# Attention: output halves joined by an accumulating transfer, and one maximum of 768 columns at the unit's end

## Chip, cores and metric

One NeuronCore of a Trainium2 chip. The metric is the device time of one execution in microseconds (us).

## The reference

A transformer block on an input of 48 x 48 positions (2304 tokens) and 384 channels, in fp32: layer norm, attention with 12 heads of 32 channels and decomposed relative positions, projection, residual; then layer norm and a mixture of 8 experts with the best 2 gates. What matters here is the attention:

```python
qkv = x @ qkv_w + qkv_b            # x: layer norm of the input, 2304 tokens
q, k, v = ...                      # 12 heads, 32 channels each
attn = einsum('bqd,bkd->bqk', q * scale, k)
bias = rel_h[..., :, None] + rel_w[..., None, :]      # from q and two tables
attn = softmax(attn + bias, axis=-1)                  # 2304 x 2304 per head
out = einsum('bqk,bkd->bqd', attn, v)
return out @ proj_w + proj_b
```

## The kernel before, in words

The stages run one after another: q, k and v with layer norm; relative-position products; attention (`phase_attention`); projection; gates; experts. Only `phase_attention` changes.

**Precision.** Values are kept as a high part in fp32r and the rest as a low part. The values of v stand as 65 columns per key tile: 32 of high parts, 32 of low parts, and one of ones for the softmax's sum (`VW = 2 * HD + 1`). So the output of a head in `o_t` has 65 rows, and the rows 0 to 31 and 32 to 63 must be added: that is the join of the halves.

**Units.** A head has 3 query blocks of 768 queries (`QB`), and each block goes over 18 key tiles of 128 keys (`TILES`): 54 units a head, 648 in all. For a unit TensorE does, in its own order written out in `head`: the scores of the unit three later (`scores`, four matmuls of 384 columns into `ps_s`, two PSUM buffers), the product of the unit's weights with v (`pv`, four matmuls into `ps_o`, high and low weights), and two matmuls of 384 columns for the row maxima of later queries (`half`, into `ps_m`). These belong to the next head's maxima, 42 of 54 units ahead (`chunk_at`, `SHIFT = 12`); the last head has them in its first 12 units only. In the last unit of a block `pv` comes ahead of the scores.

**ScalarE** takes each unit's scores twice: exp to `p_hi` (L846) and exp to `p_f` (L852), whose two buffers come free by `lo_done` of the unit two earlier. **The low part** `p_lo = p_f - p_hi` (`low`, L598) is VectorE's for two units of three, and POOL's for every third (`POOL_EVERY = 3`). `pv` waits for it. VectorE's `head` takes the maximum of the first half (`reduce_half`, L897), then the low part of the unit two later, then the maximum of the second half. `negated` (L892) makes the negative maximum of a block once in 18 units; TensorE transposes it (L757) in the unit three before a block's end, inside `scores`, ScalarE copies it (L848) between its two exponentials, SP stores it (L642) and loads it into `query_rest` (`load_max`).

**The end of a block.** ScalarE and VectorE copy one half of the columns each from `ps_o` to `o_t` (L861, L912); two buffers `o_t`. POOL's `joined` runs after its low part of the sixth unit of the next block: it copies the rows 32 to 63 to `o_low` (L719) and adds them to the rows 0 to 31 in `o_s` (L721). SP stores `o_s` to `o_d` and the row of sums to `sums_d` (`store`, L650 and L651), after `load_max` of the same block.

**SP** issues all transfers of the stage in one order: `rest(h)` loads keys and values of the next head, then, for each block, `load_rest` (about 2.1 MB, the queries with low parts, each read for six variants), `load_max` and `store`; `start` loads the next but one head's `query_hi` and `key_hi`. All of it is on one hardware queue.

Of the kernel before, what the change touches and what calls it, by code (L numbers as in the profile page):

```python
# [21 lines left out]
HEADS = 12  # L22
# [488 lines left out]
def phase_attention(nc, qk_hi_d, qk_lo_d, rel_hi_d, rel_lo_d, v_d, m_d, o_d, sums_d, key_hi0, key_rest0, room):  # L511
# [11 lines left out]
    with ExitStack() as ctx:  # L523
# [22 lines left out]
        o_low = [sb(f"o_low{i}", [HD, 2, TB]) for i in range(2)]  # L546
        o_s = [sb(f"o_s{i}", [HD, 2, TB]) for i in range(2)]
# [23 lines left out]
        o_go = sem("o_go")  # L571
        low_moved = sem("low_moved")
        o_sum = sem("o_sum")
        ot_out = [sem(f"ot_out{i}") for i in range(2)]
        all_in = sem("all_in")
# [33 lines left out]
        def _(sp):  # L609
# [44 lines left out]
            def start(h, par, last=False):  # L654
                if not last:

                    sp.wait_ge(s_ok, UNITS * h + LEAD)
                    load_hi(h + 1, 1 - par)
                load_max(h, 2)
# [24 lines left out]
            start(0, 0)  # L684
# [4 lines left out]
            for g in range(2):  # L689
                sp.wait_ge(ot_out[g], 32 + 32 * QBLOCKS * OALL_HEADS // 2)  # L690
# [5 lines left out]
            for g in range(2):  # L696
                sp.wait_ge(ot_out[g], 32 + 32 * QBLOCKS * HEADS // 2)
# [3 lines left out]
        def _(pool):  # L701
            for g in range(2):
                pool.sem_inc(ot_out[g], 32)
# [6 lines left out]
            def joined(h, par, b, last_one):  # L710

                g = (QBLOCKS * par + b) % 2
# [10 lines left out]
            FIRST = 3 * POOL_EVERY  # L723

            def head(h, par, last=False):
                for idx in range(FIRST - 1, UNITS + FIRST - 1, POOL_EVERY):
# [13 lines left out]
            head(HEADS - 1, 1, last=True)  # L740

        @block.tensor
        def _(pe):
# [32 lines left out]
            def head(h, par, last=False):  # L776
                for k in range(UNITS):
# [61 lines left out]
        def _(act):  # L839
# [14 lines left out]
            def head(h, par, last=False):  # L854
                for k in range(UNITS):
                    if k % TILES == TILES - 1:
# [3 lines left out]
                        act.wait_ge(ot_out[g], out_count(h, par, b))  # L860
# [4 lines left out]

            def out_count(h, par, b):
                return 32 * ((QBLOCKS * par + b) // 2) + 32 * QBLOCKS * half(h, par) + 32

            def half(h, par):
                return (h - par) // 2  # L870
# [16 lines left out]
        def _(dve):  # L887
# [6 lines left out]
            def reduce_half(count, s, c):  # L894
                dve.wait_ge(mm_ok, 2 * count + c + 1)
                col = s % 3 * 2 + c
                dve.tensor_reduce(mx[s // TILES][:, s // 3 % 6, col:col + 1], ps_m[:, c, 0:TB], AX.X, ALU.max).then_inc(mx_ok, 1)  # L897

            def reduce_both(s, ps):
                dve.wait_ge(mm_ok, 2 * s + 2)  # L900
                col = s % 3 * 2
                dve.tensor_reduce(mx[s // TILES][:, s // 3 % 6, col:col + 2], ps[:, :, 0:TB], AX.X, ALU.max).then_inc(mx_ok, 2)
                negated(s, s)

            def head(h, par, last=False):
                for k in range(UNITS):
                    if k % TILES == TILES - 1:
# [3 lines left out]
                        dve.wait_ge(ot_out[g], out_count(h, par, b))  # L911
# [4 lines left out]
                    if maxima:  # L916
                        reduce_half(number, s, 0)
# [7 lines left out]
            def out_count(h, par, b):  # L925
                return 32 * ((QBLOCKS * par + b) // 2) + 32 * QBLOCKS * half(h, par) + 32

            def half(h, par):
                return (h - par) // 2
# [3 lines left out]
            for s in range(UNITS - SHIFT):  # L933
                reduce_both(s, [ps_m, ps_s[:, 0:2, :], ps_s[:, 2:4, :]][s % 3])
# [960 lines left out]
```

## Time and profile before

| | us |
|---|---|
| median of 3 runs | 2444.59 |
| lowest and highest | 2442.36, 2445.06 |
| profiled execution, its own time | 2443.99 |
| profiled execution, its span | 2442.2 |

| engine | busy us | share of the span |
|---|---|---|
| TensorE | 2083.4 | 85% |
| TensorE weight loads (beside it) | 1821.8 | 75% |
| VectorE | 1536.9 | 63% |
| ScalarE | 1505.6 | 62% |
| POOL (GpSimd) | 984.6 | 40% |

The attention runs from about 340 to 1625 us of the span. Shares over the whole span average stages with different limits, so the argument needs the views of that stage. In the timelines a row is one instruction or several alike (x2), with its start, its time, engine, line, and what it writes and reads; in brackets stands the idle time of the engine ahead of it and who ended it. A matmul's row is longer than the time to the next, since matmuls overlap.

### The profile page before, as it was taken

Reading aid. Unit: us, or ns where it says so; the run is one execution under the profiler, and the core shown is the slowest. Engines: PE = TensorE matmul, PEld = TensorE weight load, DVE = VectorE, ACT = ScalarE, POOL = GpSimd, SP = SyncE. Lnnn points to the kernel's source line nnn. Section 1 sums busy time; section 2 is a strip of 40 time slices with the busy share of each in tenths; the row PEclk is TensorE's granted clock in tenths of the full one; section 3 lists DMA queues with packets and bytes.
Section 4 is the critical chain, followed back from the end, with each engine's and each line's share of the span. In section 5 each row is a group of like instructions: output and inputs, shape, how many; then the busy total and the mean of one; then the engine's idle time right before and its main releaser. Section 6 shows DMA issues by size and latency. Waiting matters only on the chain. (4 is left out here: it accounts for less than half of the span.)

```text
span 2442.2 us, 34255 instructions
## 1 busy us (share of the span) xinstructions
PE 2083.4 (85%) x11132; PEld 1821.8 (75%) x11132; DVE 1536.9 (63%) x2321; ACT 1505.6 (62%) x2533; POOL 984.6 (40%) x645
## 2 busy tenths in 40 slices
PE   7833259999999999999999999967579999999998
PEld 7822138888888888888888888746368888989997
DVE  5555368989999898999988989747633426030000
ACT  3344308877787778777877877851235555555554
POOL 0020023434443443444344434447055656565553
PEclk9955559999999999999999999978679999999999
DMA  6788783444553554446345543333143435121111
GB/s 207 234 163 197 158 158 81 88 93 81 97 113 63 106 101 93 78 86 120 74 89 99 97 94 66 91 120 116 60 138 104 126 96 169 27 56 30 27 27 20
DMA packets 90710, 247.01 MB, mean 101 GB/s; under 512 B 8824, under 2 KB 43096, under 8 KB 85156
## 3 DMA queue, kind: packets, MB, share of 16 engines
q1 hardware_dynamic: 80640, 227.11, 40.5%
q0 software_dynamic: 8944, 16.91, 4.0%
q8 instruction: 101, 1.65, 0.3%
q10 hardware_dynamic: 960, 0.80, 0.1%
q14 instruction: 65, 0.53, 0.1%
HBM read 182.81 MB, written 61.98 MB: 100 GB/s over the span
## 5 line engine op out<-in xcount | busy, mean ns | idle before, releaser
L897 DVE TENSOR_REDUCE mx<-ps_m 128x1 f32<-128x384 f32 x1212 | 644.7, 552 | 110.7 <-PE ps_m L748 102.5
L598 POOL TENSOR_TENSOR p_lo<-p_f,p_hi 128x768 fp32r<-128x768 f32 x216 | 397.8, 1842 | 764.9 <-ACT p_f L852 764.9
L846 ACT ACTIVATE p_hi<-ps_s 128x768 fp32r<-128x768 f32 x648 | 528.3, 815 | 176.3 <-PE ps_s L762 172.8
L852 ACT ACTIVATE p_f<-ps_s 128x768 f32<-128x768 f32 x648 | 525.5, 811 | 62.8 <-DVE p_lo L598 60.0
L748 PE MATMUL ps_m<-key_hi,query_hi 128*128 128x384 f32 x1240 | 430.7, 354 | 122.4 <-DVE mx L897 81.5
L598 DVE TENSOR_TENSOR p_lo<-p_f,p_hi 128x768 fp32r<-128x768 f32 x432 | 508.5, 1177 | 37.6 <-ACT p_f L852 36.6
L748 PEld LDWEIGHTS ps_m<-key_hi,query_hi 128*128 128x128 f32 x1240 | 237.0, 193 | 179.1 <-DVE mx L897 106.5
L759 PE MATMUL ps_s<-query_hi,key_hi 128*128 128x384 f32 x1296 | 341.6, 345 | 11.4 <-DMA query_rest<-m_d 9.3
L772 PE MATMUL ps_o<-p_hi,val 128*65 128x384 f32 x1296 | 335.7, 340 | 3.9 <-POOL p_lo L598 3.7
L762 PE MATMUL ps_s<-query_rest,key_rest 121*128 121x384 f32 x1296 | 335.8, 341 | 0.0
L772 PE MATMUL ps_o<-p_lo,val 128*65 128x384 f32 x1296 | 334.9, 340 | 0.0
L1675 POOL TENSOR_TENSOR h_lo<-h_f,h_hi 128x512 fp32r<-128x512 f32 x129 | 185.6, 1438 | 258.7 <-ACT h_hi L1803 256.4
L759 PEld LDWEIGHTS ps_s<-query_hi,key_hi 128*128 128x128 f32 x1296 | 234.5, 191 | 21.0 <-issue 10.3
L762 PEld LDWEIGHTS ps_s<-query_rest,key_rest 121*128 121x128 f32 x1296 | 241.0, 192 | 0.0
L1787 ACT COPY z_sb<-ps_z 128x512 f32<-128x512 f32 x129 | 75.7, 587 | 265.9 <-PE ps_z L1729 265.9
L1729 PE MATMUL ps_z<-w_ring,xg_hi 128*128 x774 | 223.8, 397 | 4.7 <-POOL xg_lo L1671 4.7
L1750 PE MATMUL ps_o<-w_ring,h_hi 128*128 x1032 | 214.5, 350 | 11.7 <-POOL h_lo L1675 11.7
L772 PEld LDWEIGHTS ps_o<-p_lo,val 128*65 128x65 f32 x1296 | 177.6, 137 | 52.1
L772 PEld LDWEIGHTS ps_o<-p_hi,val 128*65 128x65 f32 x1296 | 178.5, 138 | 31.5 <-POOL p_lo L598 5.6
L1750 PEld LDWEIGHTS ps_o<-w_ring,h_hi 128*128 128x128 f32 x1032 | 175.5, 188 | 15.2 <-issue 15.2
L1729 PEld LDWEIGHTS ps_z<-w_ring,xg_hi 128*128 128x128 f32 x774 | 144.7, 189 | 28.9 <-issue 5.1
L1797 ACT ACTIVATE h_f<-ps_h,b_sb 128x128 f32<-128x128 f32 x516 | 147.8, 369 | 6.3 <-issue 0.8
(247 smaller groups left out, 2355.0 us busy)
## 6 DMA issues: line engine op xcount, KB each, us to landing
query_rest<-rel_lo_d SPq DMA_DIRECT2D x36, 864.0 KB
query_rest<-qk_lo_d SPq DMA_DIRECT2D x36, 576.0 KB
query_rest<-qk_hi_d SPq DMA_DIRECT2D x36, 576.0 KB
rel_lo_d<-out_lo SPq DMA_DIRECT2D x6, 1728.0 KB, 33.1
query_hi<-rel_hi_d SPq DMA_DIRECT2D x12, 864.0 KB, 18.5
w_raw__19855<-w_u SPq DMA_DIRECT2D x12, 768.0 KB, 5.3
w_raw__19856<-w_u SPq DMA_DIRECT2D x12, 768.0 KB, 4.6
w_raw__19857<-w_u SPq DMA_DIRECT2D x12, 768.0 KB, 4.4
```

The costliest lines, as they stand in the source:

```text
L598: engine.tensor_tensor(p_lo[r][:], p_f[idx % 2], p_hi[r][:].bitcast(F32), ALU.subtract).then_inc(lo_done(0, idx)[0], 1)
L748: pe.matmul(ps[:, c, 0:TB], query_hi[tp][:, tile], key_hi[tp][:, keys], start=True, stop=True).then_inc(mm_ok, 1)
L759: pe.matmul(ps_s[:, bank + c, 0:TB], key_hi[par][:, j * P:(j + 1) * P], query_hi[par][:, b * QB + c * TB:b * QB + (c + 1) * TB], start=Tru ...
L762: last = pe.matmul(ps_s[:, bank + c, 0:TB], key_rest[par][:, j * P:(j + 1) * P], query_rest[b][:, j // 3, c * TB:(c + 1) * TB], start=Fals ...
L772: last = pe.matmul(ps_o[0:VW, c, 0:TB], val[par][:, j, :], part[r][:, c, :], start=(j == 0 and part is p_hi), stop=(j == TILES - 1 and par ...
L846: act.activation(p_hi[r][:], ps_s[:, bank:bank + 2, 0:TB], ACT.Exp).then_inc(hi_ok, 1)
L852: act.activation(p_f[idx % 2], ps_s[:, bank:bank + 2, 0:TB], ACT.Exp).then_inc(f_ok, 1)
L897: dve.tensor_reduce(mx[s // TILES][:, s // 3 % 6, col:col + 1], ps_m[:, c, 0:TB], AX.X, ALU.max).then_inc(mx_ok, 1)
L1675: pool.tensor_tensor(h_lo[u % H_RING][:], h_f[u % 2][:], h_hi[u % H_RING][:].bitcast(F32), ALU.subtract).then_inc(hlo_ok, 1)
L1729: last = pe.matmul(ps_z[:, u % 2, :], v[s % 2][:, k, :], moe.ring[:, cols], start=(n == 0), stop=(n == 8))
L1750: last = pe.matmul(ps_o[:, s % 2, 0:C], v[u % H_RING][:, b, :], moe.ring[:, cols], start=(c == 0 and n == 0), stop=(c == CHUNKS - 1 and n ...
L1797: last = act.activation(h_f[u % 2][:, b, :], ps_h[:, u % 2, b, :], ACT.Gelu, bias=bias)
```

## The change

Two parts. First, POOL's copy and sum and the buffers `o_low` and `o_s` go. SP stores the high rows of `o_t` to `o_d` right after the block's two copies, ahead of `load_max` and behind `load_rest`; when they have landed (`high_out`), POOL issues a transfer that adds the low rows of `o_t` to the same place in `o_d` (`accum_op`), after its low part of the ninth unit of the next block (`JOIN = 8`). The copies to `o_t` wait for that transfer (`low_out`) of the block two before. Second, TensorE issues both matmuls for the maxima at the unit's end, behind one wait, and VectorE takes one maximum of both (`reduce_both`, 768 columns), with the low part after it.

```diff
             def store(h, par, b):
                 g = (QBLOCKS * par + b) % 2
-                sp.wait_ge(o_sum, QBLOCKS * h + b + 1)
-                sp.dma_start(o_d[bass.ds(h * HD, HD), b * QB:(b + 1) * QB], o_s[g][:].rearrange("r c n -> r (c n)")).then_inc(ot_out[g], 16)
+                sp.wait_ge(acc_a, QBLOCKS * h + b + 2)
+                sp.wait_ge(acc_d, QBLOCKS * h + b + 2)
+                sp.dma_start(o_d[bass.ds(h * HD, HD), b * QB:(b + 1) * QB], o_t[g][0:HD, :, :].rearrange("r c n -> r (c n)")).then_inc(high_out[g], 16)
...
                     sp.wait_ge(s_ok, UNITS * h + TILES * (b + 1))
                     load_rest(h + 1, b)
+                    store(h, par, b)
                     if b < 2:
                         load_max(h + 1, b)
-                        store(h, par, b)
-                start(h + 1, 1 - par, h == HEADS - 2)
-                store(h, par, 2)
+                if h < HEADS - 2:
+                    sp.wait_ge(s_ok, UNITS * (h + 1) + LEAD)
+                    load_hi(h + 2, par)
+                load_max(h + 1, 2)
...
-                pool.wait_ge(acc_a, QBLOCKS * h + b + 2)
-                pool.wait_ge(acc_d, QBLOCKS * h + b + 2)
-
-                pool.wait_ge(*lo_done(h + (b == QBLOCKS - 1), (TILES * (b + 1) + 2 * POOL_EVERY - 1) % UNITS) if not last_one else lo_done(h, UNITS - 1))
-                pool.sem_inc(o_go, 1)
-                pool.tensor_copy(o_low[g][:], o_t[g][HD:2 * HD, :, :]).then_inc(low_moved, 1)
-                pool.wait_ge(low_moved, QBLOCKS * h + b + 1)
-                pool.tensor_tensor(o_s[g][:], o_t[g][0:HD, :, :], o_low[g][:], ALU.add).then_inc(o_sum, 1)
+            def joined(n):
+
+                h, b = n // QBLOCKS, n % QBLOCKS
+                g = n % 2
+                pool.wait_ge(high_out[g], 16 * (n // 2) + 16)
+                pool.dma_start(o_d[h * HD:(h + 1) * HD, b * QB:(b + 1) * QB], o_t[g][HD:2 * HD, :, :].rearrange("r c n -> r (c n)"),
+                               accum_op=ALU.add).then_inc(low_out[g], 16)
...
-                    for b in range(QBLOCKS):
-                        if idx == TILES * (b + 1) + 2 * POOL_EVERY - 1:
-                            joined(h, par, b, last and b == QBLOCKS - 1)
+                    n = QBLOCKS * h + idx // TILES - 1
+                    if idx % TILES == JOIN and idx < UNITS and n >= 0:
+                        joined(n)
...
                     if maxima:
                         if s == 0:
-
                             pe.wait_ge(hi_in[tp], 48 * ((h + 1) // 2 + 1))
 
-                        pe.wait_ge(mx_ok, number - 1)
-                        half(tp, s, 0, ps_m)
...
                     if maxima:
                         pe.wait_ge(mx_ok, number)
-                        half(tp, s, 1, ps_m)
+                        for c in range(2):
+                            half(tp, s, c, ps_m)
...
                         act.wait_ge(pv_ok, UNITS * h + k + 1 + RING)
-                        act.wait_ge(ot_out[g], out_count(h, par, b))
+                        if QBLOCKS * h + b >= 2:
+                            act.wait_ge(ot_out[g], 16 * ((QBLOCKS * h + b) // 2))
+                            act.wait_ge(low_out[g], 16 * ((QBLOCKS * h + b) // 2))
                         act.copy(o_t[g][:, 0, :], ps_o[0:VW, 0, 0:TB]).then_inc(acc_a, 1)
...
-            def reduce_both(s, ps):
-                dve.wait_ge(mm_ok, 2 * s + 2)
+            def reduce_both(count, s, ps):
+                dve.wait_ge(mm_ok, 2 * count + 2)
                 col = s % 3 * 2
                 dve.tensor_reduce(mx[s // TILES][:, s // 3 % 6, col:col + 2], ps[:, :, 0:TB], AX.X, ALU.max).then_inc(mx_ok, 2)
...
                     if maxima:
-                        reduce_half(number, s, 0)
+                        reduce_both(number, s, ps_m)
                     up, idx = unit_at(par, k, LOW_LEAD)
                     if not (last and up != par) and idx % POOL_EVERY < POOL_EVERY - 1:
                         low(dve, UNITS * h + k + LOW_LEAD, up, idx)
                     if maxima:
-                        reduce_half(number, s, 1)
                         negated(number, s)
```

VectorE's copy to `o_t` gets the same two waits as ScalarE's.

## Rows read from the trace of the kernel before

**Rows 1.** Two stretches of one block: span, busy times, granted clock, DMA share, GB/s.
```profile
963.03:997.67 34.64, 32.17 (x183) 28.44 (x182) 31.82 (x51) 27.91 (x39) 14.26 (x8) 1.00 0.37 68
1066.99:1103.27 36.28, 33.82 (x183) 29.82 (x182) 32.07 (x51) 27.87 (x39) 14.29 (x8) 0.95 0.36 65
```
**Rows 2.** Waits, 380 to 1560 us: who for whom, us in total, times, longest.
```profile
PE ps_m L748 <- DVE mx L897: 81.5, 66, 2.3
```
**Rows 3.** Timeline of undisturbed units: start, us, engine, line, operation.
```profile
1018.80 0.34 PE L748 MATMUL ps_m<-key_hi,query_hi 128*128 128x384 f32 x1
...
1019.00 0.81 ACT L846 ACTIVATE p_hi<-ps_s 128x768 fp32r<-128x768 f32 x1 [0.85 <-PE ps_s L762]
1019.17 0.56 DVE L897 TENSOR_REDUCE mx<-ps_m 128x1 f32<-128x384 f32 x1 [0.31 <-PE ps_m L748]
...
1019.71 0.81 ACT L852 ACTIVATE p_f<-ps_s 128x768 f32<-128x768 f32 x1
...
1021.44 0.81 ACT L852 ACTIVATE p_f<-ps_s 128x768 f32<-128x768 f32 x1
1021.45 0.95 DVE L598 TENSOR_TENSOR p_lo<-p_f,p_hi 128x768 fp32r<-128x768 f32 x1
1021.58 0.51 PE L759 MATMUL ps_s<-query_hi,key_hi 128*128 128x384 f32 x2
...
1022.31 1.02 DVE L897 TENSOR_REDUCE mx<-ps_m 128x1 f32<-128x384 f32 x2
1022.33 1.84 POOL L598 TENSOR_TENSOR p_lo<-p_f,p_hi 128x768 fp32r<-128x768 f32 x1 [5.85 <-ACT p_f L852]
...
1023.33 0.52 PE L759 MATMUL ps_s<-query_hi,key_hi 128*128 128x384 f32 x2
```
**Rows 4.** Timeline behind a join on POOL.
```profile
1013.86 3.44 DVE L598 TENSOR_TENSOR p_lo<-p_f,p_hi 128x768 fp32r<-128x768 f32 x1
...
1014.67 1.81 POOL L598 TENSOR_TENSOR p_lo<-p_f,p_hi 128x768 fp32r<-128x768 f32 x1
...
1017.33 0.81 ACT L852 ACTIVATE p_f<-ps_s 128x768 f32<-128x768 f32 x1 [1.81 <-DVE p_lo L598]
1017.82 0.45 PE L748 MATMUL ps_m<-key_hi,query_hi 128*128 128x384 f32 x1 [2.27 <-DVE mx L897]
```
**Rows 5.** Tile `o_t`, 380 to 1560 us: times, ns min/median/max, first and last start.
```profile
L721 POOL TENSOR_TENSOR o_s<-o_t,o_low x33: 2417/2433/2445, 415.0 to 1539.0; 32x768 f32<-32x768 f32 x33
```
**Rows 6.** Timeline at a block's turn.
```profile
1002.16 0.54 DVE L912 COPY o_t<-ps_o 65x384 f32<-65x384 f32 x1
...
1004.73 0.45 PE L748 MATMUL ps_m<-key_hi,query_hi 128*128 128x384 f32 x1 [0.20 <-DVE mx L897]
```
**Rows 7.** Timeline: second halves before and after the transposed maxima.
```profile
1030.15 0.33 PE L748 MATMUL ps_m<-key_hi,query_hi 128*128 128x384 f32 x1
...
1032.03 0.34 PE L748 MATMUL ps_m<-key_hi,query_hi 128*128 128x384 f32 x1
```
**Rows 8.** Tile `out` (experts), from 1600 us: POOL's accumulating transfers, issue ns, landing us.
```profile
L1680 POOL DMA_INDIRECT out<-y_sb,sidx x43: 1560/1594/2124, 1825.9 to 2433.7; - x43
...
DMA to landing us min/median/max: 3.0/4.2/5.7
```
**Rows 9.** A stretch of 4 us behind the loads of a head's first block.
```profile
1050.00:1054.00 4.00, 1.72 (x10) 1.39 (x9) 3.62 (x5) 1.32 (x3) 1.16 (x1) 1.00 0.81 100
```
**Rows 10.** Tile `mx`, 340 to 460 us: maxima of 768 columns ahead of the first head.
```profile
L902 DVE TENSOR_REDUCE mx<-ps_m x7: 947/948/949, 340.4 to 356.2; 128x2 f32<-128x768 f32 x7
```
**Rows 11.** Timeline of the experts: two-input operations of VectorE and POOL that start close together.
```profile
1797.52 2.74 DVE L1035 TENSOR_TENSOR w_ring<-w_raw__19855,w_ring 128x1536 fp32r<-128x1536 f32 x1
1797.63 1.00 POOL L1671 TENSOR_TENSOR xg_lo<-xg_f,xg_hi 128x384 fp32r<-128x384 f32 x1
...
1803.83 1.76 DVE L1035 TENSOR_TENSOR w_ring<-w_raw__19857,w_ring 128x1536 fp32r<-128x1536 f32 x1
1804.12 2.33 POOL L1671 TENSOR_TENSOR xg_lo<-xg_f,xg_hi 128x384 fp32r<-128x384 f32 x1 [5.49 <-ACT xg_f L1782]
```

More of the change, by code:

```diff
@@ L545, in phase_attention @@
         o_t = [sb(f"o_t{i}", [VW, 2, TB]) for i in range(2)]
-        o_low = [sb(f"o_low{i}", [HD, 2, TB]) for i in range(2)]
-        o_s = [sb(f"o_s{i}", [HD, 2, TB]) for i in range(2)]
         ps_s = ctx.enter_context(nc.psum_tensor("ps_s", [P, 4, 512], F32))
@@ L570, in phase_attention @@
         acc_d = sem("acc_d")
-        o_go = sem("o_go")
-        low_moved = sem("low_moved")
-        o_sum = sem("o_sum")
+        high_out = [sem(f"high_out{i}") for i in range(2)]
         ot_out = [sem(f"ot_out{i}") for i in range(2)]
+        low_out = [sem(f"low_out{i}") for i in range(2)]
         all_in = sem("all_in")
@@ L648, in store @@
                 g = (QBLOCKS * par + b) % 2
-                sp.wait_ge(o_sum, QBLOCKS * h + b + 1)
-                sp.dma_start(o_d[bass.ds(h * HD, HD), b * QB:(b + 1) * QB], o_s[g][:].rearrange("r c n -> r (c n)")).then_inc(ot_out[g], 16)
+                sp.wait_ge(acc_a, QBLOCKS * h + b + 2)
+                sp.wait_ge(acc_d, QBLOCKS * h + b + 2)
+                sp.dma_start(o_d[bass.ds(h * HD, HD), b * QB:(b + 1) * QB], o_t[g][0:HD, :, :].rearrange("r c n -> r (c n)")).then_inc(high_out[g], 16)
                 sp.dma_start(sums_d[bass.ds(h, 1), b * QB:(b + 1) * QB],
                              o_t[g][VW - 1:VW, :, :].rearrange("r c n -> r (c n)")).then_inc(ot_out[g], 16)
[L654 to L659, printed above, removed]
             def rest(h, par):
@@ L683, in _ @@
             sp.wait_ge(hot_ok, HOT_STEPS)
-            start(0, 0)
+            sp.wait_ge(s_ok, LEAD)
+            load_hi(1, 1)
+            load_max(0, 2)
             for h in range(loop_heads):
@@ L689, in _ @@
             for g in range(2):
-                sp.wait_ge(ot_out[g], 32 + 32 * QBLOCKS * OALL_HEADS // 2)
+                sp.wait_ge(ot_out[g], 16 * QBLOCKS * OALL_HEADS // 2)
+                sp.wait_ge(low_out[g], 16 * QBLOCKS * OALL_HEADS // 2)
             for c in range(KC):
@@ L696, in _ @@
             for g in range(2):
-                sp.wait_ge(ot_out[g], 32 + 32 * QBLOCKS * HEADS // 2)
+                sp.wait_ge(ot_out[g], 16 * QBLOCKS * HEADS // 2)
+                sp.wait_ge(low_out[g], 16 * QBLOCKS * HEADS // 2)
             sp.wait_ge(all_in, 16 * KC)
@@ L701, in _ @@
         def _(pool):
-            for g in range(2):
-                pool.sem_inc(ot_out[g], 32)
             pool.memset(ident[:], 0.0).then_inc(ident_ok, 1)
@@ L708, in _ @@
             one_hots(pool, key_hi[1], key_rest[1], hot, hot_ok)
[L710 to L721 removed]
+            def joined(n):
[4 more added lines that the diff above has]
+                               accum_op=ALU.add).then_inc(low_out[g], 16)
             FIRST = 3 * POOL_EVERY
+            JOIN = 8
             def head(h, par, last=False):
@@ L740, in _ @@
             head(HEADS - 1, 1, last=True)
+            joined(QBLOCKS * HEADS - 1)
         @block.tensor
@@ L864, in head @@
                         exps(h + (up != par), up, idx, turned_at(k, last))
[L866 to L870, printed above, removed]
             act.sem_inc(acc_a, 1)
@@ L892, in negated @@
                     dve.tensor_reduce(neg_m[s // TILES][:], mx[s // TILES][:], AX.X, ALU.max, negate=True).then_inc(neg_ok, 1)
[L894 to L897, printed above, removed]
-            def reduce_both(s, ps):
-                dve.wait_ge(mm_ok, 2 * s + 2)
+            def reduce_both(count, s, ps):
+                dve.wait_ge(mm_ok, 2 * count + 2)
                 col = s % 3 * 2
                 dve.tensor_reduce(mx[s // TILES][:, s // 3 % 6, col:col + 2], ps[:, :, 0:TB], AX.X, ALU.max).then_inc(mx_ok, 2)
-                negated(s, s)
             def head(h, par, last=False):
@@ L910, in head @@
                         dve.wait_ge(pv_ok, UNITS * h + k + 1 + RING)
-                        dve.wait_ge(ot_out[g], out_count(h, par, b))
+                        if QBLOCKS * h + b >= 2:
+                            dve.wait_ge(ot_out[g], 16 * ((QBLOCKS * h + b) // 2))
+                            dve.wait_ge(low_out[g], 16 * ((QBLOCKS * h + b) // 2))
                         dve.tensor_copy(o_t[g][:, 1, :], ps_o[0:VW, 1, 0:TB]).then_inc(acc_d, 1)
@@ L921, in head @@
                     if maxima:
-                        reduce_half(number, s, 1)
                         negated(number, s)
[L925 to L929, printed above, removed]
             dve.sem_inc(acc_d, 1)
@@ L933, in _ @@
             for s in range(UNITS - SHIFT):
-                reduce_both(s, [ps_m, ps_s[:, 0:2, :], ps_s[:, 2:4, :]][s % 3])
+                reduce_both(s, s, [ps_m, ps_s[:, 0:2, :], ps_s[:, 2:4, :]][s % 3])
+                negated(s, s)
             for idx in range(LOW_LEAD):
```

## The prediction

> **What bounds the kernel now.** I read the table of stretches first, because the change lies only in the attention stage. One block of 18 units, from one store of row maxima to the next, takes 34.64 us at a granted clock of 1.00, with TensorE busy for 32.17 us [rows 1]. The waits come next: TensorE's largest in this stage is for VectorE's maxima, 81.5 us in 66 waits, two in each of 33 blocks [rows 2]. Then the timeline, for what ends those waits. Undisturbed, a unit takes 1.75 us (scores at 1021.58 and 1023.33), which is 10 matmuls of 0.175, and TensorE never waits [rows 3]. So maxima as such are not the bound. 18 units are 31.5 us; the missing 3.14 us of a block are three disturbances:
>
> - The join of the output halves on POOL. VectorE's subtraction begins at 1013.86 and ends at 1017.30 in place of 0.95 later, and TensorE stands for 2.27 us [rows 4]. POOL's low part (1014.67 to 1016.48) had gone before it, behind the join's sum of 2.43 us [rows 4, 5]; VectorE ended 0.82 after POOL. Two-input subtractions on the two engines exclude each other.
> - The block's turn, where VectorE copies 0.54 us of output between its other work: a wait of 0.20 us is shown at the matmul after it [rows 6].
> - The transposed maxima: second half to second half 1.88 us instead of 1.75, so 0.13 [rows 7].
>
> Join and turn together therefore cost 34.64 - 31.50 - 0.13 = 3.01 us a block. Some blocks take longer: 36.28 us at a mean granted clock of 0.95, part of it at 1.2 GHz of the 2.4 [rows 1]. The 33 joins are 35.13 us apart on average (415.0 to 1539.0 in 32 steps) [rows 5], 0.49 more than 34.64, so the halved clock costs about 15.6 us in all.
>
> **The join, part by part.** Removed are 36 copies and 36 sums on POOL, 33 of them beside maxima. That takes away the 3.01 us less what the turn keeps: 33 x 3.01 = 99.3 us go. Added is one accumulating transfer a block, issued by POOL, for which the trace has only indirect ones, 1.59 us median, 1.56 to 2.12 [rows 8]. POOL has a low part every third unit, so every 5.25 us, and it takes 1.84 [rows 3], which leaves 3.4 us: the issue costs nothing, with at most 0 as gain. It waits for the high half's store, which on SP now stands behind the next head's big loads instead of ahead of them. In the worst block those keep the transfer engines busy for a share of 0.81 up to 1054 [rows 9]. POOL gets to that join 9 units, 4.8 us and the stalls below after the block's transposed maxima at 1030.15 [rows 7], about 1054.4; a wait of 1 us or so fits under the 3.4 less 1.6. At worst one block in three loses 1 us, 0 to 11 us; I take 0, since the cover is there. SP has queued behind the store only the next head's first loads and a row of maxima that isn't ready before. At the end of the stage the last join goes from 0.82 + 2.43 us of POOL to an issue of 1.59 with a landing of 4.2 [rows 5, 8] behind a store; I take 2 us more (0 to 4). In the last head, which mostly has no maxima, I take 2 us less.
>
> **The maximum, part by part.** One maximum of 768 columns takes 0.948 us [rows 10] instead of two of 0.55; instructions of VectorE back to back begin about 0.08 before their predecessor ends (1021.45 + 0.95 against 1022.31) [rows 3], so it is 0.87 of VectorE against two times 0.47. The work is near nothing less. What counts is the place. The maximum can begin only after both matmuls at the unit's end, and the subtraction, which stood between the two halves' maxima, comes after it. Time from the first scores matmul of a unit: the last of 10 matmuls starts at 1.575, its maximum 0.37 later (1018.80 to 1019.17) [rows 3], the subtraction at 1.95 + 0.87 = 2.82, ending at 3.77. In the old order it begins at about 1.6 (1021.45 in the unit begun 1.75 before 1021.58). VectorE needs 0.87 + 0.87 = 1.74 of 1.75: it fits with 0.01 to spare. The maximum ends at 2.90, TensorE wants it at 3.15. Fine as well.
>
> ScalarE's second exponential, which needs the buffer that this subtraction frees, starts 0.03 after its end (1017.30 to 1017.33) [rows 4], takes 0.81, and POOL starts 0.08 later (1022.25 to 1022.33) [rows 3]. So every third unit POOL's low part starts 0.95 + 0.03 + 0.81 + 0.08 - 1.75 = **0.12 us after** a subtraction of VectorE has begun. In the kernel before the two never meet. If VectorE goes first nothing is lost: POOL ends by 5.6 and its product is due at 5.95. If POOL goes first, it ends at 2.94 + 1.84 = 4.78, VectorE at 5.60, its next maximum at 5.52 + 0.95 = 6.47, and the halves start 0.15 later at 6.62 where 4.90 was due: **1.72 us**. Three places:
>
> - Transposed maxima: the matmuls come 0.13 later, ScalarE doesn't. 0.12 - 0.13: level, POOL first by 0.01. Price 1.72 - 0.13 = 1.59.
> - The turn, counted from the last half of the block's seventeenth unit: VectorE's maximum at 0.37, subtraction 1.24, copy 2.11, maximum 2.57, subtraction 3.44. TensorE goes on with the product and the scores, whose last matmul, the eighth, starts at 1.40; the exponentials follow at 1.77 and 2.48 (0.71 apart, 1019.00 to 1019.71) [rows 3], POOL at 2.48 + 0.81 + 0.08 = 3.37. POOL first by 0.07. The turn itself keeps 0.36 (maximum ends 3.52, halves at 3.68, due 3.32), and since POOL starts 3.37 - 0.18 = 3.19 into its unit, 0.25 later than the 2.94 above, the loss costs 1.72 + 0.25 - 0.36 = 1.61.
> - Four further meetings of a block, at 0.12.
>
> Who wins at 0.12? Two pairs of rows stand on its two sides: VectorE 0.11 us ahead (1797.52, 1797.63) was blocked and took 2.74 instead of 1.76, VectorE 0.29 ahead went first (1803.83, 1804.12) and POOL waited [rows 11]. The first case is impure: POOL had just ended another instruction, and back-to-back POOL instructions also pass a waiting VectorE [rows 4]. I take it that VectorE holds its place at 0.12 and keep the other end for the range.
>
> The Trainium skill, page "SBUF — State Buffer", section "Who interferes with whom", says that the shared port pair is an exclusive lock and goes to whoever issues first. By that rule the steady meetings are safe and both others are lost, which is my forecast; the 1797.52 row doesn't agree with it.
>
> **Sum**, on the profiled execution (2443.99 us, span 2442.2): less 99.3; plus 33 x (0.36 + 1.61 + 1.59) = 117.5; clock less 15.6, of which I give back 8, since stalls of 1.6 us come twice a block where 2.27 came once and nothing here shows whether they lower it (0 to 30); ends -2 and +2. 2443.99 + 10.6 = 2455. The median of the runs is 0.6 higher than the profiled one, which changes nothing.
>
> **Rivals.**
>
> 1. POOL also wins steady meetings. For it: the 1797.52 row. Against: its impurity. It decides from a lead needed by VectorE of over 0.12. Price 33 x 4 x 1.72 = 227 us: 2682 if all are lost. If starts scatter by more than what decides it, a share of them goes either way, 2500 to 2640. 0.24 for all, 0.20 for some.
> 2. The level meeting at the transposed maxima goes to VectorE: 33 x 1.59 less, and 4 of clock: 2399. 0.14.
> 3. VectorE wins at the turn too: 2399 - 53 - 4 = 2342. It needs VectorE to win from 0.07 behind. 0.05.
> 4. The stores land late and POOL's join holds its low part up (the change moves the wait instead of removing it): 11 us more at the bound above, more if the loads take longer: 2466 to 2500. 0.03.
>
> **Numbers.** My forecast has 0.34, with its own range 2436 to 2490 by clock and ends. About 0.2% is what a measurement can tell from no change, 2439.7 to 2449.5. Faster: 0.14 + 0.05 + 0.07 of the forecast's low end = 0.26. Same: 0.08 of it. Slower: 0.24 + 0.20 + 0.03 + 0.19 = 0.66. The range from 2395 to 2695 leaves out rival 3 and the edges.
>
> **What would show it.** After, POOL's sum and copy are gone; TensorE's waits for maxima are two a block, 1.4 to 1.6 us long, at the turn and at the transposed maxima, each with a subtraction of about 2.6 us on VectorE. A block is then about 35.1 us. If it is about 42, with a long subtraction every third unit, rival 1 holds; 32 would be rival 3. Long waits of POOL for the store before the join would be rival 4. A maximum well over 0.95 us would make the whole count wrong.

## The result and the profile after

The changed kernel takes 2352.43 us (median of 4 runs, 2351.75 to 2361.22) against 2443.58 (2442.36 to 2445.06) measured beside it: a ratio of 0.9635, 95% interval 0.9611 to 0.9659. It is 91 us faster where the forecast was 11 slower. The profiled execution is the slowest of the four, 2361.22 us with a span of 2359.1; it stands against 2443.99 and 2442.2 of before.

The costliest groups on VectorE and POOL (line, engine, operation, count | busy us, mean ns | idle before, releaser):

```profile
L595 POOL TENSOR_TENSOR p_lo<-p_f,p_hi 128x768 fp32r<-128x768 f32 x216 | 531.8, 2462 | 606.3 <-ACT p_f L840 606.3
L881 DVE TENSOR_REDUCE mx<-ps_m 128x2 f32<-128x768 f32 x620 | 592.4, 956 | 209.4 <-PE ps_m L738 207.0
...
L595 DVE TENSOR_TENSOR p_lo<-p_f,p_hi 128x768 fp32r<-128x768 f32 x432 | 424.1, 982 | 38.1 <-ACT p_f L840 37.0
```

POOL's low part is stretched to 2.46 us on average (1.84 undisturbed), VectorE's is not: 0.98, where an undisturbed one takes 0.95. So the meetings do take place, nearly every time, and POOL is the one that waits.

Stretches from one store of row maxima to the next (stretch: us, then busy us of PE, PEld, DVE, ACT, POOL, the granted clock, DMA share, GB/s): first 33 blocks in one, then a plain block, a block in which VectorE loses one meeting, and the block in which POOL's join waits longest. They answer to [rows 1].

```profile
397.89:1479.29 1081.40, 1060.20 (x5972) 919.76 (x5971) 912.68 (x1056) 920.71 (x1255) 518.38 (x231) 1.00 0.54 101
990.06:1022.15 32.09, 31.91 (x183) 27.75 (x182) 27.34 (x33) 27.92 (x39) 15.45 (x7) 1.00 0.56 114
1022.15:1056.11 33.96, 32.62 (x183) 27.78 (x182) 28.89 (x33) 27.89 (x40) 15.21 (x7) 1.00 0.42 73
595.02:633.61 38.59, 33.85 (x183) 29.19 (x183) 28.66 (x33) 27.87 (x39) 14.57 (x7) 0.96 0.55 95
```

A plain block takes 32.1 us instead of 34.64, 0.6 above the 31.5 of 18 undisturbed units. 33 blocks take 1081.4, which is 32.77 each, so 0.63 x 33 = 20.8 us lie in blocks longer than a plain one (32.14, the median of these). Cut at each store of row maxima, 16.5 of the 20.8 us are in ten blocks in which a join waits for its store (the fourth row has 6.45 of them), and 3.6 in two blocks that have another cause, of which the third row is one. In that row's block the join doesn't wait at all. VectorE's maximum starts 0.27 us late there, after idle time that the profile puts down to no wait ("issue"), and POOL passes it at the next steady meeting:

```profile
1049.60 0.96 DVE L881 TENSOR_REDUCE mx<-ps_m 128x2 f32<-128x768 f32 x1 [0.27 <-issue]
...
1050.25 1.84 POOL L595 TENSOR_TENSOR p_lo<-p_f,p_hi 128x768 fp32r<-128x768 f32 x1 [2.71 <-ACT p_f L840]
...
1050.47 2.43 DVE L595 TENSOR_TENSOR p_lo<-p_f,p_hi 128x768 fp32r<-128x768 f32 x1
```

The waits of the same stage (who for whom: us, times, longest); [rows 2] has no successor, since TensorE no longer waits for a maximum:

```profile
POOL o_d L708 <- DMA o_d<-o_t: 47.9, 13, 7.7
...
PE ps_o L762 <- POOL p_lo L595: 20.5, 44, 4.6
```

And the timeline from the transposed maxima through the turn (start, us, engine, line, operation):

```profile
1023.44 2.66 POOL L595 TENSOR_TENSOR p_lo<-p_f,p_hi 128x768 fp32r<-128x768 f32 x1 [2.78 <-ACT p_f L840]
1023.45 0.95 DVE L595 TENSOR_TENSOR p_lo<-p_f,p_hi 128x768 fp32r<-128x768 f32 x1
...
1025.47 0.51 PE L738 MATMUL ps_m<-key_hi,query_hi 128*128 128x384 f32 x2
...
1026.09 0.96 DVE L881 TENSOR_REDUCE mx<-ps_m 128x2 f32<-128x768 f32 x1 [0.79 <-PE ps_m L738]
...
1026.15 0.56 PE L762 MATMUL ps_o<-p_hi,val 128*65 128x384 f32 x2 [0.17 <-POOL p_lo L595]
...
1026.96 0.95 DVE L595 TENSOR_TENSOR p_lo<-p_f,p_hi 128x768 fp32r<-128x768 f32 x1
...
1027.83 0.55 DVE L892 COPY o_t<-ps_o 65x384 f32<-65x384 f32 x1
...
1028.52 0.81 ACT L840 ACTIVATE p_f<-ps_s 128x768 f32<-128x768 f32 x1
...
1029.16 0.94 DVE L595 TENSOR_TENSOR p_lo<-p_f,p_hi 128x768 fp32r<-128x768 f32 x1
...
1029.40 2.41 POOL L595 TENSOR_TENSOR p_lo<-p_f,p_hi 128x768 fp32r<-128x768 f32 x1 [3.31 <-ACT p_f L840]
```

At the first meeting POOL starts 0.01 us before VectorE and still waits. At the turn it starts 0.24 us after VectorE, not 0.07 before it.

### The profile page after: what moved, and what is told of

The parts are those of the page before. It is cut to its first block and busy times, and to the rows that moved or that the text cites. A ratio compares the mean times of both kernels' runs of the same rounds, so it can differ in the third digit from the quotient of the medians.

```text
span 2359.1 us, 34179 instructions
## 1 busy us (share of the span) xinstructions
PE 2058.6 (87%) x11132; PEld 1784.0 (76%) x11132; DVE 1393.5 (59%) x1715; ACT 1504.7 (64%) x2533; POOL 1026.6 (44%) x609
## 3 DMA queue, kind: packets, MB, share of 16 engines
q8 instruction: 101, 1.65, 0.3%
## 5 line engine op out<-in xcount | busy, mean ns | idle before, releaser
L595 POOL TENSOR_TENSOR p_lo<-p_f,p_hi 128x768 fp32r<-128x768 f32 x216 | 531.8, 2462 | 606.3 <-ACT p_f L840 606.3
L881 DVE TENSOR_REDUCE mx<-ps_m 128x2 f32<-128x768 f32 x620 | 592.4, 956 | 209.4 <-PE ps_m L738 207.0
L595 DVE TENSOR_TENSOR p_lo<-p_f,p_hi 128x768 fp32r<-128x768 f32 x432 | 424.1, 982 | 38.1 <-ACT p_f L840 37.0
L738 PE MATMUL ps_m<-key_hi,query_hi 128*128 128x384 f32 x1240 | 326.2, 344 | 40.9 <-DMA query_hi<-rel_hi_d 38.5
L738 PEld LDWEIGHTS ps_m<-key_hi,query_hi 128*128 128x128 f32 x1240 | 198.6, 190 | 101.0 <-DMA query_hi<-rel_hi_d 38.8
L762 PEld LDWEIGHTS ps_o<-p_hi,val 128*65 128x65 f32 x1296 | 173.2, 137 | 60.9 <-POOL p_lo L595 34.7
L469 PE MATMUL ps<-q_sb,tab 96*48 96x192 f32 x288 | 60.3, 365 | 106.0 <-DMA q_sb<-qk_lo_d 63.5
```

Source lines behind the costliest of these rows:

```text
L595: engine.tensor_tensor(p_lo[r][:], p_f[idx % 2], p_hi[r][:].bitcast(F32), ALU.subtract).then_inc(lo_done(0, idx)[0], 1)
L738: pe.matmul(ps[:, c, 0:TB], query_hi[tp][:, tile], key_hi[tp][:, keys], start=True, stop=True).then_inc(mm_ok, 1)
L762: last = pe.matmul(ps_o[0:VW, c, 0:TB], val[par][:, j, :], part[r][:, c, :], start=(j == 0 and part is p_hi), stop=(j == TILES - 1 and par ...
```

## Experiments

Lags below are POOL's start less VectorE's start, from the trace's start times to the nanosecond, for every pair of low parts that overlap; a "lost" meeting is one in which VectorE's subtraction took over 1.2 us. The 12 or 13 lost ones at the end of the last head, where no maxima run, are not counted. A steady meeting is one away from the turn and from the transposed maxima.

**Which half of the change brings the time?** First the join alone: the maxima stay where they were.

```diff
+                        pe.wait_ge(mx_ok, number - 1)
+                        half(tp, s, 0, ps_m)
...
-                        for c in range(2):
-                            half(tp, s, c, ps_m)
+                        half(tp, s, 1, ps_m)
...
-                        reduce_both(number, s, ps_m)
+                        reduce_half(number, s, 0)
...
+                        reduce_half(number, s, 1)
```

> Only the join is changed (accumulating DMA, new order on SP); the maxima stay two of 384, one in the middle of the unit. Theory A (the join's lock on VectorE was nearly all there was to gain, and the new place of the maximum costs at most the turn): VectorE's subtraction no longer stands 3.4 us behind POOL's sum, blocks near 31.5 + 0.13 + 0.3 = 31.9 us, and once a head a wait of about 1 to 2 us for the store as in the changed kernel: 2345 to 2360 us. Rival B (the maxima bring a good part of the 91 us, because with them the low part waits less for other work): over 2375 us.

Measured: 2352.63 us, ratio 0.9626 (0.9610 to 0.9642), the same as the whole change as far as the two intervals can tell. Theory A holds.

Then the maxima alone, with POOL's copy and sum kept (the same lines the other way round, in the kernel before).

> Only the maxima are changed (one of 768 columns, both matmuls at the unit's end); POOL keeps its copy and sum of 2.43 us. Theory A: the stall behind the join stays (about 2.3 us of TensorE a block), the meetings with POOL every third unit go to VectorE, which is 0.12 us ahead: 2435 to 2460 us. Rival B (the merged maximum gives slack by itself): under 2420 us. Rival C (with POOL's join beside it the meetings after it go to POOL for some units): over 2475 us.

Measured: 2464.62 us, ratio 1.0081 (1.0062 to 1.0101), 5 us beyond theory A's bound. The stall behind the join is still there:

```profile
1024.10 2.44 POOL L721 TENSOR_TENSOR o_s<-o_t,o_low 32x768 f32<-32x768 f32 x1
...
1025.63 3.50 DVE L598 TENSOR_TENSOR p_lo<-p_f,p_hi 128x768 fp32r<-128x768 f32 x1
1026.51 1.80 POOL L598 TENSOR_TENSOR p_lo<-p_f,p_hi 128x768 fp32r<-128x768 f32 x1
...
1029.18 0.57 PE L772 MATMUL ps_o<-p_hi,val 128*65 128x384 f32 x2 [2.08 <-DVE p_lo L598]
```

It is [rows 4] again: POOL's next low part, directly behind its sum, passes the subtraction that has waited since 1025.63. TensorE now misses the product instead of a maximum, for 2.08 us. Plain blocks take 34.74 us (34.64 before), and one with a stretch of halved clock 36.59 (36.28 before); of the 33 blocks 15 took over 36 us (first exponential to first exponential) where before it was 10. The two stretches:

```profile
1042.81:1077.55 34.74, 32.45 (x183) 27.76 (x182) 29.99 (x33) 27.93 (x40) 17.68 (x8) 1.00 0.51 102
1077.55:1114.14 36.59, 34.28 (x183) 29.09 (x182) 30.47 (x33) 27.92 (x40) 17.00 (x8) 0.95 0.35 65
```

So the merged maximum is worth nothing that shows beside the new join, and costs 23 us beside the old one (2464.62 less 2441.3, the kernel before in the same runs). Why it costs so much there was only partly found: 3.3 us are the 0.10 of each plain block, and the clock fell in 14 of the blocks instead of 10; the rest stays open.

**Is merging needed?** The changed kernel with two maxima of 384 behind both matmuls:

```diff
-                        reduce_both(number, s, ps_m)
+                        reduce_half(number, s, 0)
+                        reduce_half(number, s, 1)
```

> The changed kernel, but with two maxima of 384 columns back to back behind both matmuls in place of one of 768. 0.07 us more of VectorE in each unit; two units of three then ask 0.94 + 0.87 = 1.81 of it, the third 0.94, so on average it fits 1.75. The subtraction beside POOL's low part starts some 0.06 later, so its lead is 0.04 to 0.1 instead of 0.12. Theory A (VectorE goes first as long as it isn't behind by more than about 0.1): 2352 to 2362 us. Rival B (the merging is needed: the lead is used up and POOL goes first, up to four to six times a block at 1.7 us each): 2500 us or more.

Measured: 2347.17 us, ratio 0.9609 (0.9593 to 0.9625): rival B falls, and it is 5 us under theory A's range, though its interval overlaps the changed kernel's. The first of the two maxima starts before the second matmul has ended, so VectorE's subtraction starts 1.14 us after the unit's last matmul and not 1.32 (medians at the turn in this form and in the changed one). The steady lag goes from 0.12 to 0.08, as expected, and VectorE stays first.

**Is the join's wait for the high store worth removing?** All stores ahead of `load_rest` on SP, and the join three units later:

```diff
-            JOIN = 8
+            JOIN = 11
...
+                    store(h, par, b)
                     load_rest(h + 1, b)
-                    store(h, par, b)
```

> The changed kernel with the store of the high half put ahead of the next head's load_rest on SP's queue, and POOL's join three units later (5.25 us). Theory A (about 15 us of the changed kernel are POOL's waits for that store, once a head, and part of the clock behind the 4.56 us stall): the waits of TensorE for POOL's low part at these places are gone, 2335 to 2345 us. Rival B (the waits were hidden or come back as waits of the output copies for their buffer, which is now freed later): 2350 to 2356 us.

Measured: 2360.22 us (2355.13 to 2370.72), ratio 0.9678 (0.9651 to 0.9705): no gain, by the medians 8 us slower than the changed kernel, with intervals that just overlap. Neither theory named what came. POOL's waits in the 33 blocks are gone, but `query_hi` for the head after next comes late:

```profile
PE ps_o L762 <- DMA query_hi<-rel_hi_d: 9.3, 10, 1.4
```

In both kernels `load_hi` stands behind the third block's store on SP. What the edit moved is `load_rest`, which now also waits for that store. So SP issues the last of `load_hi` 10.6 us behind the block's store of row maxima instead of 7.5 (861.41 less 850.79, and 867.89 less 860.37), and it lands 17.4 us after its issue in place of 15.6 (medians). The edit moved the join too, so the run doesn't price the two parts one by one.

**What is a lost meeting worth, and where is the point of decision?** The forecast rests on both. An extra maximum on VectorE, of a constant tile and with its result unused, delays the subtraction that meets POOL, by its width:

```diff
                     if not (last and up != par) and idx % POOL_EVERY < POOL_EVERY - 1:
+                        if idx % POOL_EVERY == 1:
+                            dve.tensor_reduce(spare_mx[:, 0:1], ident[:, 0:8], AX.X, ALU.max)
```

> The changed kernel with one small extra maximum (8 columns of a constant tile, result unused) on VectorE ahead of the subtraction that meets POOL's low part (unit index 1 modulo 3). It delays that subtraction by an estimated 0.07 to 0.1 us, so POOL's low part now starts 0.02 to 0.05 after it instead of 0.12. Theory A (VectorE goes first as long as POOL isn't clearly ahead, by more than about 0.1 us): 2352 to 2362 us, every subtraction 0.95 us. Rival B (the forecast's: a lead under about 0.1 is lost): 2500 to 2640 us, subtractions of about 2.6 us every third unit.

> As before, with a maximum of 64 columns: 0.14 us or so, POOL and VectorE level or POOL 0.02 ahead. Theory A: 2352 to 2365 us still. Rival B: over 2500 us.

> As before, with a maximum of 128 columns: 0.2 us, POOL 0.08 ahead. Theory A: this is near the point of decision, some meetings go to POOL: 2360 to 2600 us, and the trace's pairs tell where it lies. Rival B: over 2550 us.

> As before, with two maxima of 128 columns: 0.4 us, POOL 0.3 ahead in every steady meeting. Theories A and B alike: POOL goes first, the subtraction takes 2.4 to 2.6 us, and each of four to six meetings a block costs about 1.7 us as the prediction worked out: 2352 + 33 x 5 x 1.7 = 2630 us (2570 to 2690). Rival C (the price was overrated, since the ring of four products and the two buffers of the exponential take up part of the stall): under 2500 us.

| extra columns | time, us | over 2352.4 | steady lag, us | lost meetings | us for each |
|---|---|---|---|---|---|
| 8 | 2411.87 | 59.4 | +0.03 to +0.07 | 36 of 201 | 1.65 |
| 64 | 2444.36 | 91.9 | -0.03 to +0.02 | 51 of 202 | 1.80 |
| 128 | 2646.56 | 294.1 | -0.10 to -0.06 | 170 of 202 | 1.73 |
| 2 x 128 | 2690.88 | 338.5 | -0.30 to -0.25 | 202 of 202 | 1.68 |

The price is near the predicted one (1.59 to 1.72). The last column divides the whole difference, in which the changed kernel's late stores and the extra maximum's own time stand too. Plain blocks leave the stores out: 34.05 less 32.14 is 1.91 us for one meeting, at the transposed maxima, with 8 columns, and 42.53 less 32.14 is 1.73 for each of six with 2 x 128. Theory A's mechanism holds and its figure doesn't: the point of decision is not at 0.1 but very sharp and almost at zero. Over the traces of the changed kernel and its twelve relatives here, 184 meetings with a lag of -0.023 to -0.001 went to VectorE, and all 32 with -0.060 to -0.024 to POOL (one more, at -0.023 in the run with the join alone, went to POOL, whose low part there stood right behind its DMA issue). The cut is as sharp as that in one trace alone: from -0.028 to -0.015 there are meetings only in the run with 64 columns and that one exception. Two meetings of the run with 64 columns, one on each side:

```profile
980.76 2.68 POOL L596 TENSOR_TENSOR p_lo<-p_f,p_hi 128x768 fp32r<-128x768 f32 x1 [2.69 <-ACT p_f L841]
980.78 0.95 DVE L596 TENSOR_TENSOR p_lo<-p_f,p_hi 128x768 fp32r<-128x768 f32 x1
...
991.47 1.83 POOL L596 TENSOR_TENSOR p_lo<-p_f,p_hi 128x768 fp32r<-128x768 f32 x1 [2.68 <-ACT p_f L841]
991.49 2.62 DVE L596 TENSOR_TENSOR p_lo<-p_f,p_hi 128x768 fp32r<-128x768 f32 x1
```

My expectations by theory A were wrong for the first three all the same (2411.87 against at most 2362, 2444.36 against at most 2365, 2646.56 against at most 2600), and the fourth is at the edge (2690.88 against 2690). I had looked at the steady meetings, which with 8 columns all stay with VectorE; the level one at the transposed maxima went to -0.07 and is lost once in every block:

```profile
982.50 1.84 POOL L596 TENSOR_TENSOR p_lo<-p_f,p_hi 128x768 fp32r<-128x768 f32 x1 [2.77 <-ACT p_f L841]
982.51 0.15 DVE L902 TENSOR_REDUCE spare_mx<-ident 128x1 f32<-128x8 f32 x1
982.58 2.58 DVE L596 TENSOR_TENSOR p_lo<-p_f,p_hi 128x768 fp32r<-128x768 f32 x1
...
985.21 0.56 PE L763 MATMUL ps_o<-p_hi,val 128*65 128x384 f32 x2 [1.24 <-DVE p_lo L596]
```

The turn is an exception to the sharp point. In the same run POOL starts 0.22 us ahead there and waits, in 31 of 32 cases:

```profile
989.00 0.94 DVE L882 TENSOR_REDUCE mx<-ps_m 128x2 f32<-128x768 f32 x1
989.71 2.87 POOL L596 TENSOR_TENSOR p_lo<-p_f,p_hi 128x768 fp32r<-128x768 f32 x1 [5.37 <-ACT p_f L841]
989.87 0.15 DVE L902 TENSOR_REDUCE spare_mx<-ident 128x1 f32<-128x8 f32 x1
989.93 0.95 DVE L596 TENSOR_TENSOR p_lo<-p_f,p_hi 128x768 fp32r<-128x768 f32 x1
```

With 64 columns (0.28 ahead) it is again 31 of 32, with 128 (0.35) 32 of 33; with two of 128 (0.54) POOL wins all. What makes the turn different wasn't found. In it, and not in the others, VectorE's maximum follows a copy without a pause, and POOL starts while that maximum still has 0.23 us to run. That alone doesn't decide it: with two of 128 POOL starts at the same point of that maximum and wins.

The Trainium skill, page "SBUF — State Buffer", section "Who interferes with whom", calls the port pair that the two share an exclusive lock; this case's traces agree: wherever two low parts overlap by more than 0.16 us, one of them ends late, VectorE's with over 1.0 us in place of 0.95 or POOL's with over 1.9 in place of 1.84. That it goes to whoever issues first, as I took it in the prediction, agrees with the steady meetings up to 0.023 us of recorded start, and not with the turn, nor with the meeting behind POOL's sum in the run with the maxima alone, which VectorE lost in all 33 blocks with a lead of 0.87 us.

**Why is POOL 0.24 late at the turn?** I took the transposition for the cause and moved it by one unit:

```diff
-        turn_at = {TILES + SHIFT + 2: 0, 2 * TILES + SHIFT + 2: 1, SHIFT + 2: 2}
+        turn_at = {TILES + SHIFT + 1: 0, 2 * TILES + SHIFT + 1: 1, SHIFT + 1: 2}
```

> The changed kernel with the transposition of the block's maxima one unit earlier, away from the unit whose low part is POOL's. Theory A (at the transposed maxima the meeting is level because TensorE and so VectorE come 0.13 late and ScalarE doesn't; POOL, second, then ends so late that the product of the block's last unit waits 0.17 us, which is why POOL comes 0.24 behind VectorE at the turn and not 0.07 ahead): that meeting is now at about +0.1 like the others, the wait before the last product goes to under 0.1 us, the turn's meeting comes down to between 0 and +0.15, VectorE still first. 2345 to 2353 us. Rival B (the 0.24 at the turn has nothing to do with it): the turn's meeting stays at +0.22 to +0.26. Rival C (the turn's meeting falls below -0.05): POOL goes first there, 33 x 1.6 more: about 2405 us.

Measured: 2361.55 us, ratio 0.9668 (0.9652 to 0.9684), 9 us above the changed kernel with intervals that just overlap (a plain block took 32.57 us for 32.14), and the turn's lag stays at 0.22 to 0.28: rival B. The meeting at the transposition did move to +0.12, but the product waits as before:

```profile
1015.76 2.53 POOL L595 TENSOR_TENSOR p_lo<-p_f,p_hi 128x768 fp32r<-128x768 f32 x1 [3.35 <-ACT p_f L840]
1017.83 0.34 PE L738 MATMUL ps_m<-key_hi,query_hi 128*128 128x384 f32 x1
...
1018.34 0.56 PE L762 MATMUL ps_o<-p_hi,val 128*65 128x384 f32 x2 [0.18 <-POOL p_lo L595]
```

Counted from the last matmul of maxima before it, POOL's low part ends at 0.467 and the product starts at 0.520 us; in the changed kernel 0.462 and 0.516 (medians of 36 turns). POOL started earlier against it (-2.06 for -2.19) and ended no earlier, because its end hangs on VectorE's. This fits that being second at all makes POOL late, by whatever lag. The run with 8 extra columns bears it out from the other side: there POOL goes first at the transposed maxima, and at the turn it starts 0.22 us ahead of a subtraction that the extra maximum delays by 0.07, where it was 0.24 behind. In the run with the join alone, where nobody meets, the product starts at 0.176, right after that matmul:

```profile
1018.20 1.85 POOL L595 TENSOR_TENSOR p_lo<-p_f,p_hi 128x768 fp32r<-128x768 f32 x1 [3.58 <-ACT p_f L841]
...
1020.64 0.34 PE L738 MATMUL ps_m<-key_hi,query_hi 128*128 128x384 f32 x1
...
1020.82 0.51 PE L762 MATMUL ps_o<-p_hi,val 128*65 128x384 f32 x2
```

That the shift cost time has its own cause: the transposition now waits for its maxima.

```profile
PE ps_s L747 <- DVE neg_m L876: 13.2, 34, 1.8
```

**A version under both kernels.** Only the first block's store goes ahead of `load_rest`:

```diff
+                    if b == 0:
+                        store(h, par, b)
                     load_rest(h + 1, b)
-                    store(h, par, b)
+                    if b > 0:
+                        store(h, par, b)
```

> The changed kernel, but on SP the store of a head's first block goes ahead of the next head's load_rest (for the other two blocks it stays behind; POOL's join stays where it is). Theory A (POOL's waits for this store, once a head, are what makes that head's second block 33.4 to 37.2 us instead of 32.1, some 15 to 20 us in all; loads for the head after next are not late as they were with all stores in front): no wait of TensorE for POOL's low part over 0.5 us, 2333 to 2343 us. Rival B (the store is slow by itself, or load_rest becomes late): within 5 us of the changed kernel's 2352.

Measured: 2348.84 us, ratio 0.9617 (0.9601 to 0.9633), between the theories: its interval overlaps the changed kernel's, so by time alone this isn't settled. In the profile it is: TensorE's waits for POOL from 380 to 1500 us are 6.5 us in 35, the longest 0.3, where they were 18.9 in 42, the longest 4.6. Two steady meetings were still lost, with POOL 0.23 and 0.24 ahead (two blocks of 33.9 us), as in the changed kernel's trace. Both come behind a maximum that starts 0.28 us late after "issue" idle, as at 1049.60 above. The three traces with two maxima of 384 behind both matmuls have no such pause in the stage, and what causes it stays open.

With two maxima of 384 in addition:

> The same store order, with two maxima of 384 columns back to back in place of one of 768. With two maxima alone the run was at 0.9609 of the kernel before, the changed kernel at 0.9635. Theory A (the two gains add up): 2328 to 2338 us, under both kernels. Rival B (what the two maxima gained was in the same waits): as the run with the store order alone, within 3 us.

Measured: 2339.14 us (2338.53 to 2339.39), ratio 0.9575 (0.9559 to 0.9591), 1 us above theory A's bound. Its interval lies below that of the changed kernel. Of the 9.7 us under the run with the store order alone about 6 are TensorE's waits for POOL (0.4 us for 6.5, since POOL, second at the transposed maxima, now ends earlier and the product starts 0.347 us after the last maxima's matmul instead of 0.52), and 2 are its waits behind the two lost meetings. All 33 blocks are now alike, with TensorE busy for 1057.06 of 1057.33 us:

```profile
396.81:1454.14 1057.33, 1057.06 (x5972) 941.63 (x5971) 934.38 (x1648) 931.96 (x1255) 532.87 (x231) 1.00 0.54 103
973.62:1005.63 32.01, 32.01 (x183) 28.53 (x182) 28.33 (x51) 28.20 (x40) 16.14 (x7) 1.00 0.56 114
```

All three edits together:

> All three: two maxima of 384, the first block's store ahead of load_rest, the transposition one unit earlier. Lags of the steady meetings are 0.08 with two maxima, of the turn 0.18 to 0.2. Theory A (every meeting stays above the point of decision, which the delayed kernels put at 0.02 to 0.04 us of POOL's lead): 2325 to 2336 us. Rival B (with two maxima the turn's meeting has less room and falls below that point): 33 x 1.6 more, about 2385 us.

Measured: 2352.11 us, ratio 0.9632 (0.9616 to 0.9648). No meeting was lost (steady lags 0.08, the turn's 0.18 to 0.24), so rival B is out, and so is theory A's time: blocks take 32.4 us, with the late transposition as above.

## Why the prediction was wrong, point by point

**The bound.** Right: the join held VectorE, and taking it off POOL gave back nearly all. The join alone gives the whole 0.9626. Gain of a plain block: 34.64 - 32.14 = 2.50 us, so 82.5 us in 33, of the 3.01 and 99.3 that the join and the turn had cost.

**Lost meeting at the transposed maxima (33 x 1.59 = 52.5 us).** This step failed. The sum put POOL ahead by 0.01, and the trace has lags of -0.012 to +0.035 (40 pairs, most within 0.01 of zero): the time of the meeting was right to about 0.01 us. What was wrong is to take the sign of so small a number for the outcome. VectorE wins down to -0.023. The forecast's own rival 2 was this, at 0.14; between a level meeting's two outcomes the rows gave no reason to prefer either, so that the trace fell on the good side was not foreseeable from them.

**Lost meeting at the turn (33 x 1.61 = 53.1 us).** This failed too, and for a reason that could have been read before. The sentence "its product is due at 5.95" holds for units whose product follows the scores. In a block's last unit TensorE takes the product ahead of them, 4 x 0.175 = 0.70 earlier, so it is due at 5.25, and a POOL that comes second ends at about 5.5 (2.82 + 2.65). The product then starts 0.34 us late (0.516 for 0.176), and with it the scores, both exponentials and POOL's next low part: 3.76 instead of the forecast's 3.37, while VectorE is only 0.07 later than worked out (3.52 for 3.44). -0.07 became +0.24. And the -0.07 would probably not have lost anyway: in the run with 8 columns, where the meeting at the transposed maxima is lost as forecast, POOL is 0.22 ahead at the turn and waits.

**The turn's own cost (0.36).** A plain block is 32.14 - 31.50 - 0.13 = 0.51 above the undisturbed units. The size was underrated by 0.15, 5 us in all. The wait of the last product is part of what was missing: the fastest version (two maxima of 384), in which TensorE doesn't wait for it, has blocks of 32.05, which is 0.09 less.

**The price of a lost meeting (1.72).** Right within a fifth: 1.65 to 1.80 in four runs by the whole time, 1.73 and 1.91 by plain blocks. Rival 1's sum for all meetings lost was 2682 us; the run in which all are lost took 2690.88. That rival had 0.24 and needed a point of decision above 0.12; the row at 1797.52 in [rows 11], on which it stood, doesn't show the steady case. A POOL instruction directly behind another behaves differently, as [rows 4] already said and the run with the maxima alone repeats.

**The join's wait (0, bound 11).** The place was right, "one block in three", the size was not. It is 16.5 us in the profiled execution, with one wait of POOL of 7.71 us for the high half's store and a stall of 4.56:

```profile
622.84 0.78 POOL L708 DMA_DIRECT2D o_d<-o_t  x1 [7.71 <-DMA o_d<-o_t]
...
625.50 0.56 PE L762 MATMUL ps_o<-p_hi,val 128*65 128x384 f32 x2 [4.56 <-POOL p_lo L595]
```

The issue was misread in the other direction: it takes 0.78 us, not the 1.59 of the indirect form in [rows 8]. The rest of the 20.8 us that longer blocks cost is 3.6 for two steady meetings lost behind "issue" idle, which no term of the sum had, and 0.7 in blocks a little over a plain one. With the store in front the waits are gone, which shows their cause. The other three executions are 9 us shorter than the traced one; whether by shorter waits can't be said from one trace.

**The clock.** I gave back 8 of 15.6 us; about 1.9 came back. Between 380 and 1530 us one stretch fell below 1.00, behind the 4.56 us stall (0.96 for its block, TensorE busy for 33.85 us instead of 31.91), and its cost is part of the 16.5. In the kernel before it fell in ten blocks, each time behind a wait of TensorE of 2.27 to 2.29 us. The run with two extra maxima of 128 shows it from the other side. Its waits, and then its stage as one stretch: with 201 waits of at most 1.7 us the clock stays at 1.00.

```profile
PE ps_o L763 <- DVE p_lo L596: 258.5, 201, 1.7
```

```profile
405.00:1860.00 1455.00, 1196.35 (x6254) 945.00 (x6252) 1277.70 (x1503) 967.64 (x1328) 410.42 (x245) 1.00 0.41 77
```

**The ends (-2, +2).** The exponentials of the stage in the changed kernel (tile `p_hi`: count, ns min/median/max, first to last start):

```profile
L834 ACT ACTIVATE p_hi<-ps_s x648: 782/807/908, 366.8 to 1531.1; 128x768 fp32r<-128x768 f32 x162
```

The last head's two blocks after the 33 gave 2.5 us (56.1 to 53.6, first exponential to first exponential). The stretch from the last unit's exponential (1531.1 for 1614.6) to the span's end is 828.0 for 827.6 us, so +0.4.

**The sum again**, on the profiled executions: 2443.99 - 82.5 (blocks) - 15.6 (clock) + 20.8 (longer blocks: 16.5 late stores, 3.6 two lost meetings, 0.7 rest) - 2.5 + 0.4 (ends) - 2.9 (the stage began at 366.8 for 369.7, which the change doesn't touch) = 2361.7, against 2361.22. That it closes so well is partly luck: counted from first exponential to first exponential the 33 blocks took 1160.3 and 1081.5 us, 1.5 more of a gain than the sum has, and the units ahead of them took 0.8 longer. The outcome is rival 3 (2342) with rival 4's wait on top, and the forecast gave these 0.05 and 0.03. The range's lower end was 2395 because rival 3 was left out.

## What to carry over

When two engines exclude each other and the schedule puts them within 0.1 us, work out both outcomes with equal chances unless a row shows that very kind of meeting, and make the price per meeting the firm part of the forecast. The engine that comes second is late by the other's whole remaining time, so look for the one consumer that wants it earlier than its siblings do. And a slow two-input operation on POOL is worth moving to a DMA if VectorE works next to it, with the queue that feeds that DMA ordered so that its source isn't behind the next stage's loads.

## What was not expected of the hardware

- The contest for the shared path is decided as sharply as the trace can show: VectorE up to 0.023 us behind POOL's recorded start, POOL from 0.024, without one exception among 216 near-level meetings in which POOL came from waiting (those next to the cut are all of one run); but at the turn VectorE wins from 0.22 to 0.35 us behind in 94 of 97 cases and loses at 0.54.
- A POOL low part directly behind another POOL instruction passes a subtraction of VectorE that began 0.87 us earlier (33 of 33 blocks with the maxima alone).
- The issue of a direct accumulating DMA takes POOL 0.76 to 1.02 us (median 0.78), half of an indirect one.
- Two maxima of 384 columns back to back take 1.02 us against 0.96 for one of 768, but the first begins 0.37 us after the first matmul (1005.43 to 1005.80 in the fastest version), the one of 768 0.62 after it (1025.47 to 1026.09 above). The subtraction behind comes 0.18 earlier, so two are the faster form here.
